# Result rows moved inside the next block's slots, smaller weight-form pieces, another opening order and later gathers in a routed feed-forward kernel

## The reference, cut to what matters

```python
# x: (64, 64, 512) f32, subj: (64,), weights: (8, 64, 64)
c = einsum('bct,bcd->bdt', x, weights[subj])     # one 64x64 map per batch row
xf = c.reshape(4096, 512)                        # tokens
probs = softmax(xf @ gate_w.T)                   # 8 experts
top_p, top_i = top_k(probs, 2)
y = sum over the 2 chosen experts e of top_p * ((silu(xf @ fc1[e].T) * (xf @ fc2[e].T)) @ proj[e].T)   # 352 wide
shared = (silu(xf @ s1.T) * (xf @ s2.T)) @ sproj.T                                                    # 1408 wide
out = x + y + sigmoid(xf @ shared_gate.T) * shared
```

## Time and profile before

| | |
|---|---|
| median of 3 runs | 1242.92 us |
| the profiled execution, its own time | 1248.33 us |
| its span | 1246.5 us |
| ScalarE, VectorE, GpSimd busy | 38%, 69%, 22% of the span |
| moved by DMA | 276.32 MB, mean 222 GB/s |

### The profile page before, as it was taken

How to read it: one execution, slowest core, us unless ns; L and a number is a source line. 1 busy time by engine, 2 the same in 40 slices (tenths; PEclk the granted TensorE clock), 3 DMA queues, 4 the chain that set the end, 5 groups by cost and what they waited for, 6 DMA issues and landing times.

```text
span 1246.5 us, 17429 instructions
## 1 busy us (share of the span) xinstructions
PE 1230.1 (99%) x6180; PEld 1024.4 (82%) x6180; DVE 854.2 (69%) x1373; ACT 468.3 (38%) x776; POOL 272.2 (22%) x372
## 2 busy tenths in 40 slices
PE   8998999999999999999999999999999999999998
PEld 6887888888889998888888888887878888888887
DVE  5555455687677777666666655677787787877865
ACT  4332332311056666555555544541232142123121
POOL 3477775000111112111111111023021300400200
PEclk9999999999999999999999999999999999999999
DMA  8688977222377677666666675289659748866552
GB/s 294 226 315 309 341 248 280 101 102 101 137 265 262 225 248 255 210 208 215 205 206 217 216 252 199 77 279 343 204 190 335 231 143 296 293 179 205 193 167 95
DMA packets 111684, 276.32 MB, mean 222 GB/s; under 512 B 11794, under 2 KB 11922, under 8 KB 106994
## 3 DMA queue, kind: packets, MB, share of 16 engines
q1 hardware_dynamic: 69330, 167.62, 38.4%
q0 software_dynamic: 14384, 57.42, 13.7%
q10 hardware_dynamic: 27888, 50.21, 12.8%
HBM read 206.53 MB, written 68.68 MB: 221 GB/s over the span
## 4 chain that ended last, share of the span: by engine, by line
PE 92%; DMA 4%; DVE 2%; issue 1%; ACT 1%; SPq 0%; DVEq 0%; ACTq 0%
PE bank_h L975 39%; PE bank_o L975 23%; PE bank_h L1229 12%; PE bank_t L1229 9%; PE bank_t L952 2%; PE bank_h L1111 2%; DMA xf_transposed<-xt 2%; PE bank_t L975 1%; PE bank_o L893 1%; PE bank_t L883 1%; DMA x_hi<-late_up 1%; DMA partial_rows<-res 1%; PE bank_h L893 1%; DMA maps<-cond_w 1%; PE bank_h L875 0%
## 5 line engine op out<-in xcount | busy, mean ns | idle before, releaser
L975 PE MATMUL bank_h<-x_hi,w_hi 128*128 128x512 f32 (+1 forms) x704 | 255.5, 363 | 0.2
L975 PE MATMUL bank_h<-x_hi,w_lo 128*128 128x512 f32 (+1 forms) x704 | 248.0, 352 | 0.0
L975 PE MATMUL bank_h<-x_lo,w_hi 128*128 128x512 f32 (+1 forms) x704 | 247.6, 352 | 0.0
L975 PE MATMUL bank_o<-wp_hi,h_hi 128*128 128x512 f32 (+1 forms) x433 | 175.9, 406 | 0.8 <-DVE res L1856 0.5
L841 POOL DMA_INDIRECT rows<-xf_rows,token_of x71 | 69.5, 978 | 489.6 <-PE bank_t L952 360.1
L975 PE MATMUL bank_o<-wp_lo,h_hi 128*128 128x512 f32 (+1 forms) x433 | 174.3, 403 | 0.0
L975 PE MATMUL bank_o<-wp_hi,h_lo 128*128 128x512 f32 (+1 forms) x433 | 173.5, 401 | 0.0
L975 PEld LDWEIGHTS bank_h<-x_hi,w_lo 128*128 128x128 f32 x704 | 133.4, 190 | 18.7
L975 PEld LDWEIGHTS bank_h<-x_hi,w_hi 128*128 128x128 f32 x704 | 133.6, 190 | 16.4 <-DVE x_lo L1795 1.1
L975 PEld LDWEIGHTS bank_h<-x_lo,w_hi 128*128 128x128 f32 x704 | 133.8, 190 | 14.9
L1933 DVE TENSOR_TENSOR w_lo<-raw,w_hi 128x640 fp32r<-128x640 f32 (+1 forms) x116 | 93.4, 834 | 24.2 <-ACT w_hi L1313 24.2
(11 more groups left out here) (269 smaller groups left out, 2424.1 us busy)
## 6 DMA issues: line engine op xcount, KB each, us to landing
raw<-ew SPq DMA_DIRECT2D x29, 1408.0 KB, 6.9
w_early<-late_up ACTq DMA_DIRECT2D x81, 256.0 KB, 3.6
slot_rows<-res SPq DMA_DIRECT2D x32, 512.0 KB, 3.2
rawp<-ewp SPq DMA_DIRECT2D x29, 512.0 KB, 7.3
x_hi<-late_up ACTq DMA_DIRECT2D x54, 256.0 KB, 3.4
x_lo<-late_up ACTq DMA_DIRECT2D x54, 256.0 KB, 3.9
late_up<-raw POOLq DMA_DIRECT2D x7, 1792.0 KB, 8.0
xt_in<-xf_transposed SPq DMA_DIRECT2D x11, 1024.0 KB, 7.2
```

The costliest lines, as they stand in the source:

```text
L975: mm = pe.matmul(dst, a, m, start=(first and i == 0), stop=(last and i == 2))
```

## The change

It does five things:

- `WARM` is 4, and SyncE issues its half of the maps and the index list ahead of tile 0.
- In blocks 1, 2 and 3 the last block's results are stored in slot 1 and the next residual rows are loaded in slot 3 (after waiting for that store), in place of both at the block's end. Block 3, the last with slots, also stores its own at its end as before.
- `late_split_sums` is done in two halves, each a copy and a subtraction of 128x512; the counts that others wait for are changed to match.
- The gathers start after the second late chunk.
- In the first late block, group 0 has the picks of tiles 0 to 4 (was 0 to 5), and group 2 those of tiles 5, 6 and 7 at rows 1, 2 and 3 (was 6 and 7 at rows 1 and 3). In the other blocks group 0 has five picks (was six) and the last is done at row 3 of group 2.

```diff
-WARM = 3
+WARM = 4
...
+            sp.dma_start(maps[0:64, :, :], cond_w.rearrange("s c d -> c s d")).then_inc(maps_in, 16)
+            sp.dma_start(subj_sb[:, :], subj).then_inc(maps_in, 16)
             front_load(0, 0)
-            sp.dma_start(subj_sb[:, :], subj).then_inc(maps_in, 16)
-            sp.dma_start(maps[0:64, :, :], cond_w.rearrange("s c d -> c s d")).then_inc(maps_in, 16)
...
                         load_xt(0, b + 1)
+                    if k == 1 and not first:
+                        store_res(0, b - 1)
+                    if k == 3 and not first:
+                        sp.wait_ge(res_stored, 16 * b)
+                        load_res(0, b)
                 if slots < SLOTS:
                     front_store_xt(TILES - 1, 1)
-                store_res(0, b)
-                sp.wait_ge(res_stored, 16 * (b + 1))
-                load_res(0, b + 1)
+                    store_res(0, b)
+                    sp.wait_ge(res_stored, 16 * (b + 1))
+                    load_res(0, b + 1)
...
-                late_split(*late_forms(slice(3, 7)), w_sums, 4 * j)
+                for half in range(2):
+                    q = slice(3 + 2 * half, 5 + 2 * half)
+                    late_split(*late_forms(q), w_sums[:, 2 * half:2 * half + 2], 5 * j + half)
...
-            pool.wait_ge(late.p_full, PRODUCTS)
+            pool.wait_ge(late.p_full, 2 * PRODUCTS)
...
-                    if r in ((0, 1, 2, 4, 5, 6) if b else (0, 2, 3, 4, 5, 6)):
-                        late_pick(HROWS * b + ((2, 3, 4, 4, 5, 6, 7)[r] if b else max(r - 1, 0)))
+                    picks_at = {0: 2, 1: 3, 3: 4, 4: 5, 6: 6} if b else {0: 0, 2: 1, 4: 2, 5: 3, 6: 4}
+                    if r in picks_at:
+                        late_pick(HROWS * b + picks_at[r])
...
-                    if b == 0 and r in (1, 3):
-                        late_pick(6 + r // 2)
+                    if b == 0 and r in (1, 2):
+                        late_pick(4 + r)
+                    if r == 3:
+                        late_pick(HROWS * b + 7)
```

More of the change, by code:

```diff
@@ L614, in _ @@
             sp.wait_ge(shared[0].w_lo, 2 * len(PARTS[0]))
-            sp.wait_ge(late.split_lo, 4 * LATE)
+            sp.wait_ge(late.split_lo, 5 * LATE)
             sp.wait_ge(late.up_stored, 16 * LATE)
@@ L762, in late_sums @@
                 pool.wait_ge(late.raw_in[j % 2], 16 * (j // 2 + 1))
-                at_least(pool, late.split_lo, 4 * j - 3)
+                at_least(pool, late.split_lo, 5 * j - 3)
                 nc.gpsimd.tensor_tensor(s1, a21, a22, ALU.add).then_inc(late.summed, 1)
@@ L784, in late_split_sums @@
                 at_least(pool, late.up_stored, 16 * j)
-                late_split(*late_forms(slice(3, 7)), w_sums, 4 * j)
+                for half in range(2):
+                    q = slice(3 + 2 * half, 5 + 2 * half)
+                    late_split(*late_forms(q), w_sums[:, 2 * half:2 * half + 2], 5 * j + half)
             def late_split_raw(j):
-                late_split(*late_forms(slice(0, 2)), raw_up[j % 2][:, :, 0, :].rearrange("p (q k) f -> p q k f", q=2), 4 * j + 1)
-                late_split(*late_forms(2), raw_up[j % 2][:, 2:4, 1, :], 4 * j + 2)
-                pool.wait_ge(late.split_lo, 4 * j + 3)
+                late_split(*late_forms(slice(0, 2)), raw_up[j % 2][:, :, 0, :].rearrange("p (q k) f -> p q k f", q=2), 5 * j + 2)
+                late_split(*late_forms(2), raw_up[j % 2][:, 2:4, 1, :], 5 * j + 3)
+                pool.wait_ge(late.split_lo, 5 * j + 4)
                 nc.gpsimd.dma_start(late_up[j], raw12[:, 2 * UP:2 * UP + PRODUCTS * SLOT]).then_inc(late.up_stored, 16)
@@ L799, in late_split_down @@
                 at_least(pool, late.down_stored, 16 * j)
-                late_split(*(down_forms[:, part, :].bitcast(F32R) for part in range(2)), down_raw, 4 * j + 3)
-                pool.wait_ge(late.split_lo, 4 * j + 4)
+                late_split(*(down_forms[:, part, :].bitcast(F32R) for part in range(2)), down_raw, 5 * j + 4)
+                pool.wait_ge(late.split_lo, 5 * j + 5)
                 nc.gpsimd.dma_start(late_down[:, :, j * C:(j + 1) * C], down_forms).then_inc(late.down_stored, 16)
@@ L807, in _ @@
                     pool.wait_ge(late.summed, 4 * j + 4)
-                    at_least(pool, late.split_lo, 4 * j + (0, 1, 3, 4)[part])
+                    at_least(pool, late.split_lo, 5 * j + (0, 2, 4, 5)[part])
                 pool.wait_ge(cond_done, t - 3)
```

## The result

The changed kernel took 1250.82 us in the median of 20 runs (1242.23 to 1255.53), the kernel before 1246.24 us in the median of 20 runs beside them (1242.52 to 1250.76). The ratio is 1.0036, with a 95% interval of 1.002 to 1.0053: about 4.5 us slower. The prediction was 1237.0 us in a range of 1233 to 1242; both the sign and the range are wrong.

What follows compares the result with a forecast made beforehand. TensorE, busy 99% of the span, bounds the kernel, so only idle or slowed time can go: opening 2.4, half the front's gain 1.9, late part 1.6, together 5.9 us off 1242.92, giving 1237.0 us, range 1233.0 to 1242.0.

Steps and rivals of the forecast that it cites:

- TensorE could then start mapping at 8.9: Opening: maps issued 0.8 us earlier let TensorE begin mapping at 8.9 us; a fourth warm-up product ends at 8.8.
- The rival that the opening does nothing: Second rival, opening: tile 0 is late or the clock falls, leaving 3.5 us of gain, 1239.4 us; chance 0.11.
- Block 1's 5.1 us: Front: block 1's excess over block 2, 55.70 against 50.60 us, taken as gone once nothing waits at the block's end.
- the third rival: Blocks 1 to 3: transposed store behind 2 MB takes over 14 us, stalling three blocks; 1249 us, chance 0.08.
- 4.3 us, with GpSimd's stores beside it perhaps 7: Front, slot 1: time for the about 1.7 MB that the transposed tile's store would find queued ahead.
- the burst behind the end-of-block wait, which made the queue long, is gone: Front: argument against the slower rival, that transfers held behind the end-of-block wait would no longer go out together.
- The tolerance of 14 us: Front, slot 1: TensorE feels the transposed tile's store only if it takes past 14 us.
- GpSimd's pace: First rival, front: late casts set the pace, front gives nothing or up to 1 us; 1239 to 1241 us, chance 0.23.
- the stall after it hides this: Block 1, slot 4: GpSimd's last cast has only 0.34 us of cover, hidden today by the following stall.
- The late part: First late block: later gathers give 3.0 us, three picks in a row cost group 2 1.4; gain 1.6 us.
- a chunk later the same surplus meets weights that are needed only after group 0's rows: Late part: gathers moved one chunk later delay only weights needed 16 us on, so chunks 1 and 2 gain 3.0 us.
- half of the front's gain: Profile to ordinary run: only 1.9 of the front's 3.8 us counted, as the profiled execution was 5.4 us above the median.

Runs made afterwards that it cites:

- e3: The kernel before with the opening alone (fourth warm-up product, maps issued first): 1240.47 us, ratio 0.9965.
- e9: The changed kernel with the sums split in one piece as before: 1248.07 us, ratio 1.0027.
- e11: The changed kernel with the next block's late token load issued one chunk earlier: 1245.53 us, ratio 1.0003.
- e10: The changed kernel with the results stored at the block's end without a wait, residual rows still loaded in slot 3: 1249.01 us, ratio 1.0029.
- e4: The kernel before with only the result rows stored and residual rows fetched inside the next block's slots: 1248.53 us, ratio 1.0022.
- e8: The kernel before with the new opening, results stored at the block's end without a wait, residual rows loaded in slot 3: 1240.34 us, ratio 0.9953.
- e13: The changed kernel with both the one-piece split and the results' store at the block's end without a wait: 1242.42 us, ratio 0.9992.
- e14: The changed kernel with one-piece split, results stored at the block's end without a wait, and tokens loaded one chunk earlier: 1240.89 us, ratio 0.9970.
- e5: The kernel before with the late part alone (later gathers and the picks' new places): 1249.02 us, ratio 1.0020.
- e2: The changed kernel with the late part (gathers' wait and picks' places) as before: 1245.55 us, ratio 0.9997.
- e6: The kernel before with only the gathers' wait changed, starting after the second late chunk: 1245.17 us, ratio 1.0006.
- e15: The changed kernel with the opening as before (three warm-up products, tile 0 ahead of the maps): 1255.42 us, ratio 1.0092.

## Why the prediction was wrong

**The opening: right mechanism, term too small.** It said 2.4 us with 3.2 as the upper bound; the first chunk starts 4.2 us earlier in the profile and e3 measures 4.4 (1.6 to 7.1). The failed step is "TensorE could then start mapping at 8.9", which has two terms. It credited the maps with 0.8 us for the earlier issue and left their landing time of 6.66 us as it was. VectorE's copy of the maps' first piece starts at 5.54 us instead of 9.36, 3.8 us earlier. The trace does not have the landing itself, but 3.8 less the 0.8 of issue leaves about 3.0 us by which the transfer, now first in its queue, was faster; the 6.66 us were those of a transfer with others ahead of it. And it priced the fourth warm-up product at the 0.91 us a matmul of the other three, to end at 8.8. The eight matmuls were through at 6.93 us in the changed kernel and at 7.93 in e3, and the first map follows them at once (6.97 and 7.77 us), with the maps already there; only in e9 and e11 does it wait 0.24 and 0.19 us more, for tile 0. The upper bound should have let both shrink. The rival that the opening does nothing falls.

**Block 1's 5.1 us: gone there, and back next door.** The text gave the threshold, a transposed store over 14 us, and the right arithmetic for it in the third rival: 13.85 plus 2.7 for the extra MB is 16.6, and 17.25 was measured in block 2. The step that failed is the queue that this store would find, "4.3 us, with GpSimd's stores beside it perhaps 7", and with it the weight given against the rival: "the burst behind the end-of-block wait, which made the queue long, is gone". The trace of the changed kernel has 13.74, 17.25 and 13.16 us from issue to landing in blocks 1, 2 and 3. The DMA engines were as busy without the burst: their share in blocks 1 and 2 is 0.85 and 0.84 where it was 0.84 in both the earlier trace rows, since the bytes are the same. The forecast moved 1 MB to directly ahead of the very store whose lateness it had read, and argued from a lull that the DMA share did not show. Rival 3 was half right: one long block, not three (block 3's store cost 0.57), and 0.08 was too little. e10 confirms its cause by moving the store alone. Over all three blocks, this store (the one issued next after the load of the transposed tiles) takes 13.2 to 17.3 us in the changed kernel, e4 and e9, which store the results in slot 1, and 4.5 to 7.2 us in e8, e10 and e13, which store them at the block's end. The tolerance of 14 us counts from the moment at which the tile is ready, not from the store's issue. In the kernel before the store took 13.85 us and TensorE lost 2.90 all the same, since VectorE had already waited 3.74 us for the tile's buffer before the store went out at 87.24.

**GpSimd's pace: the right rival, and too small.** 1.3 us in all was charged for late casts, about 0.65 a block; measured are 1.30 us in block 1 of the changed kernel alone, and 1.12 and 1.19 in successive slots of e10, where nothing else is late, with block 3, for which nothing was charged, 3.5 us longer. The prediction noted for the kernel before that "the stall after it hides this"; it did not ask what the casts would cost with the whole front on time. The two causes, undone together, are worth 5.5 us, where one at a time gave 1.1 and 0.9.

**The late part: three terms, two right, one missing.** Chunks 1 and 2 gain 3.0 us in the profiled execution, as predicted. Group 2 loses 1.5, predicted 1.4. What failed is "a chunk later the same surplus meets weights that are needed only after group 0's rows". It looked at what the gathers had delayed, the weights, and not at what stands where they were moved to. The trace of before held it: the next block's tokens were loaded at 852 us in 14.1 us, and VectorE's sum that needs them comes right after group 0. That this collision is the cause is shown by e11, which moves only the token load: chunk 3 is 9.53 us and 4.1 us are back. Its size is less sure, since chunk 3 lost only 2.4 us in the profiled execution. Taken whole, the late part (from chunk 0's start to the end) is 427.3 to 430.2 us, 428.8 in the mean, in the seven profiled executions with both late edits and the later token load, 426.4 to 428.2, 427.4 in the mean, in the six with the late part as before, and 426.0 in e11 and e14. That is a loss of 1.5 us by the profiles; by the runs it is 2.5 us (e5 alone) to 4.9 (e2, e13 against e8). So the late part lost 1.5 to 5 us where +1.6 was forecast, and where the part above 1.5 us lies no row shows.

**The way from the profile to the median.** Three runs made the profiled execution of before look 5.4 us slow; twenty say 2.1. So "half of the front's gain" for an ordinary run was still too much: e4, the rows' edit alone, is 2.7 us slower, and of the kernel before's own front three profiled executions exist, of which one (e6) has no stall to remove. What stays open is how often each stall comes in runs that were not profiled. The runs of one version differ by up to 16 us (e5), and no profile stands behind most of them. Likewise the rest of the 1.2 us between block 2 and the late part, and e15's 7.0 against e3's 4.4 us, are within what the intervals allow and have no cause shown.

In sum, by ratios, step by step from the kernel before: the opening with the end-of-block wait removed -5.9 us (e8; e3, the opening alone, -4.4), the later gathers and the picks on top of it +4.9 (e13 against e8), the store's place and the split on top of that +5.5 (the changed kernel against e13). That these make the 4.5 us measured is arithmetic, but the second has a witness of its own in e2, which undoes the same lines inside the changed kernel: also 4.9. The third has two causes, the store and the split, and how it divides between them is not shown. Each difference carries an uncertainty of some 2 to 3 us.

## What to carry to other kernels

Before moving a transfer or a gather, list what is already in flight at the place it moves to and who waits for that, not only whom it delayed where it was. Read a landing time as queue plus transfer: it shrinks or grows with what is issued ahead of it, and a store that takes 13.85 us with a 14 us tolerance has no room for one more MB. Where two waits lie in the same slots, undo both before saying that either costs nothing. And before setting out to remove a stall that one profile shows, take a second profile of the same code: of the two here, one did not have it.

## What the runs showed of the hardware that was not expected

**The same transfer, several landing times.** The 256 KB transposed store took 13.85 us right behind one 1 MB transfer in the kernel before; behind two, in the changed kernel, it took 13.74, 17.25 and 13.16. The 1 MB token load took 14.1 us with SyncE's queue at 68% of the DMA engines and 20.8 with it at 52%, though the engines moved no less in total (363 GB/s in the first stretch, 392 in the second). In this case the order of SyncE's own transfers did not protect the load from another issuer's. The Trainium skill (DMA: Bandwidth & Descriptors, "Queues, rings and completion order") says that each DMA engine goes round the queues that have work, packet by packet. The shares above are in line with it, since SyncE's fell as the gathers brought more; no run here looks at the order of single packets. e11 is what to do about it: ask for the load before the other queue fills.

**A cast that waits for the other engine.** GpSimd's cast of 64x64 takes 0.24 us (87.39), but 0.70 at 86.27. VectorE's subtraction ran from 86.12 to 86.88:

```profile
86.12 0.76 DVE L1798 TENSOR_TENSOR h_lo<-h_sb,h_hi 128x512 fp32r<-128x512 f32 x1
```

That is at most 0.46 us of the 1.30 us that TensorE then waits; no run takes it away alone. The prediction had cited the exclusive lock of the Trainium skill (SBUF — State Buffer, "two separate sides") for VectorE being held by GpSimd; here the trace agrees the other way round: the cast ends 0.09 us after the subtraction, on the path that sets the pace.

**The clock behind short gaps.** After 2.97 us of idle time in block 2 the granted clock is 0.50, the level of 1.2 GHz, for 6 us, and the next two transposes take 0.66 us where 0.38 is shown for two at 159.54; after 1.30 us in block 1 it stays at 1.00. In e13 a gap of 1.19 us, at the same map, was followed by 0.50 from 88 to 91 us, and the next map came 7.8 us later where the changed kernel has 6.2. So a gap just over 1 us can already cost more than its length, though not each time.

**The warm-up is slow first, and the clock column does not say so.** The granted clock reads 1.00 from 1 to 11 us in the kernel before. Yet in all seventeen profiled executions the first four warm-up matmuls start at 1.47, 2.48, 3.34 and 4.19 us, 0.85 us apart but for the first pair, and later ones, where the pace changes at all, 0.43 apart: the last four of the changed kernel at 5.04, 5.48, 5.91 and 6.33. The pace changed after 4.2 us in e4 and only after 6.7 in e3 and e8, and no run shows what sets the moment. Eight matmuls took from 5.2 us (e11) to 6.7 (e8) in this way, so 0.91 us was no fixed price for one more.
